# A quarter of the first sequence's probabilities split before it is turned, and turned by DMA transposes

## The reference

```
x = x + layernorm(attn(layernorm(x)))         # attn: q, k with rotary positions,
                                              #   w = softmax(q k^T / sqrt(128)), out = (w v) wo^T
x = x + layernorm(ffn(layernorm(x)))          # ffn, twice: z = z + mixed(rmsnorm(z))
# mixed: router softmax over 8 experts, best 2 of 8, each silu(z w1) * (z w3) @ w2, weighted
```

## Time and profile before

| | |
|---|---|
| median of 3 runs (lowest, highest) | 1055.57 us (1053.36, 1055.62) |
| the profiled execution's own time; its span | 1055.24 us; 1053.5 us |
| mean granted TensorE clock | 0.987 of full |
| PE busy | 994.1 us, 94% |
| DVE, ACT, POOL busy | 692.6, 563.5, 564.4 us |
| chain that ended last | PE 79%, DVE 12% |
| one step of the first sequence | 7.63 us |

### The profile page before, as it was taken

The page is one execution under the profiler, slowest core; times in us unless marked ns, Lnnn a source line. Parts: engine busy times, 40 slices in busy tenths (PEclk is TensorE's granted clock), DMA queues, the critical chain, the costliest instruction groups (busy, mean ns, idle before and its releaser), DMA issues.

```text
span 1053.5 us, 22892 instructions
## 1 busy us (share of the span) xinstructions
PE 994.1 (94%) x7304; PEld 687.3 (65%) x7304; DVE 692.6 (66%) x1511; ACT 563.5 (53%) x1107; POOL 564.4 (54%) x742
## 2 busy tenths in 40 slices
PE   7999998989999899999999999999998999999991
PEld 5678786767788567666666755666755666666661
DVE  7889998989998555684434546635469433575557
ACT  4567676668888645433334566335575333333333
POOL 3335566875788764434444366444376444455435
PEclk9999999999999999999999999999999999999996
DMA  9910000000000245324337534437434433764563
GB/s 310 370 41 0 0 0 1 1 16 21 15 16 16 48 106 119 96 71 106 90 91 178 134 96 132 95 107 178 119 105 119 98 90 92 171 173 118 146 183 133
DMA packets 137498, 105.32 MB, mean 100 GB/s; under 512 B 84673, under 2 KB 124225, under 8 KB 137409
## 3 DMA queue, kind: packets, MB, share of 16 engines
q1 hardware_dynamic: 123776, 66.88, 24.4%
q0 software_dynamic: 13632, 37.24, 12.0%
HBM read 54.27 MB, written 31.20 MB: 81 GB/s over the span
## 4 chain that ended last, share of the span: by engine, by line
PE 79%; DVE 12%; issue 3%; POOL 2%; ACT 2%; DMA 1%; SPq 0%; another core or an unknown queue 0%; ACTq 0%; DVEq 0%; POOLq 0%
PE psum_s L915 32%; PE psum_o L2242 16%; PE psum_s L1679 6%; PE psum_s L2231 6%; PE psum_t L1674 4%; PE psum_o L1719 3%; PE psum_o L1714 3%; PE psum_t L749 2%; DVE arena L1442 2%; PE psum_s L1656 1%; DMA arena<-in_rope 1%; DVE arena L1422 1%; PE psum_t L2206 1%; PE psum_o L1726 1%; PE psum_y L1706 1%
## 5 line engine op out<-in xcount | busy, mean ns | idle before, releaser
L915 PE MATMUL psum_s<-w_all,arena 128*128 x1704 | 391.9, 380 | 3.2 <-issue 2.5
L1886 POOL DMA_INDIRECT token_rows<-arena,result_row_of_row x142 | 147.9, 1041 | 297.5 <-ACT arena L1995 294.4
L915 PEld LDWEIGHTS psum_s<-w_all,arena 128*128 128x128 f16 x1704 | 157.9, 98 | 183.2 <-issue 8.6
L2242 PE MATMUL psum_o<-w_all,arena 128*128 x1704 | 209.4, 273 | 9.3 <-DVE arena L2170 8.7
L900 DVE SCALAR_TENSOR_TENSOR arena<-psum_s,gate_scale,arena 128x512 f32<-128x512 f32 x142 | 106.5, 750 | 162.8 <-ACT arena L894 78.6
L2242 PEld LDWEIGHTS psum_o<-w_all,arena 128*128 128x128 f16 x1704 | 165.1, 98 | 53.4 <-issue 14.4
L2170 DVE TENSOR_TENSOR arena<-psum_s,arena 128x512 f16<-128x512 f32 x142 | 97.9, 689 | 128.7 <-ACT arena L1988 105.9
L1995 ACT ACTIVATE arena<-psum_o 128x256 f32<-128x256 f32 x142 | 54.4, 383 | 217.4 <-PE psum_o L2242 214.5
L876 POOL DMA_INDIRECT arena<-sorted_rows,token_of_row x142 | 139.7, 984 | 46.5 <-issue 40.4
L894 ACT ACTIVATE arena<-psum_s,silu_scale 128x512 f32<-128x512 f32 x142 | 97.6, 687 | 108.7 <-PE psum_s L915 55.2
L1988 ACT ACTIVATE arena<-psum_s 128x512 f16<-128x512 f32 x142 | 84.7, 597 | 29.6 <-PE psum_s L2231 21.7
(11 more groups left out here) (320 smaller groups left out, 1362.8 us busy)
## 6 DMA issues: line engine op xcount, KB each, us to landing
arena<-token_rows SPq DMA_DIRECT2D x64, 256.0 KB, 3.9
w_all<-in_L_ffn_w SPq DMA_DIRECT2D x24, 512.0 KB, 10.0
sorted_rows<-w_all SPq DMA_DIRECT2D x24, 256.0 KB
out<-x_sb SPq DMA_DIRECT2D x7, 512.0 KB, 3.1
arena<-sorted_rows,token_of_row POOLq DMA_INDIRECT x142
arena<-arena SPq DMA_TRANSPOSE x142
token_rows<-arena,result_row_of_row POOLq DMA_INDIRECT x142
x_sb<-in_L_attn_x SPq DMA_DIRECT2D x1, 2048.0 KB, 15.5
```

The costliest lines, as they stand in the source:

```text
L915: last = nc.tensor.matmul(bank, e_xT[:, u, lx * DC + c, :], w_split[:, bass.ds(e * EW + at, FF)], start=(q == 0), stop=(q == 3 * DC - 1))
L1886: nc.gpsimd.indirect_dma_start(rows, bass.IndirectOffsetOnAxis(ap=targets[:, at : at + 1], axis=0), y_row[:, u, :], None).then_inc(s_sent[ ...
L2242: last = nc.tensor.matmul(psum_e, hT[:, lh, c, :], w_split[:, bass.ds(e * EW + at, D)], start=(q == 0), stop=(q == 3 * FC - 1))
```

## The change

**The quarter.** In the first sequence TensorE no longer turns quarter 0. ACT scales it as it stands, once into f16 (hi) and once in place (`quarter_hi`); POOL subtracts (`quarter_lo`); SP turns hi and lo by two DMA transposes of 128 x 512 f16 each into the place that the split quarter had. PE turns quarter 1 alone at the start of a step and multiplies quarter 0 at the end of the step, behind quarter 2. The buffers are single: hi of tile t-1 is written when the transposes of tile t-2 have landed, SP issues the first one when the PV product of tile t-2 is done, and the exponentials of tile t overwrite the probabilities once `quarter_lo` has read them.

```diff
@@ ACT @@
+            def quarter_hi(t):
+                act.wait_ge(s_exp, 2 * t + 1)
+                    act.wait_ge(s_split_T, 32 * t)
+                nc.scalar.activation(probs_split[:, 0, :], probs[:, 0:512], ACT.Copy, scale=P_SCALE).then_inc(s_p_hi, 1)
+                act.wait_ge(s_p_hi, 4 * t + 2)
+                nc.scalar.activation(probs[:, 0:512], probs[:, 0:512], ACT.Copy, scale=P_SCALE).then_inc(s_quarter, 1)
...
@@ POOL @@
+            def quarter_lo(t):
+                pool.wait_ge(s_quarter, t + 1)
+                nc.gpsimd.tensor_tensor(probs_split[:, 1, :], probs[:, 0:512], probs_split[:, 0, :],
+                                        ALU.subtract).then_inc(s_split_lo, 1)
...
@@ SP @@
+            for t in range(NT):
+                for l in range(2):
+                    if l:
+                        sp.wait_ge(s_split_lo, t + 1)
+                    else:
+                        sp.wait_ge(s_p_hi, 4 * t + 2)
+                        if t:
+                            sp.wait_ge(s_pv, t)
+                    sp.dma_start(pT[:, l, 0:512].rearrange("p (g t) -> p g t", g=4), probs_split[:, l, :],
+                                 transpose=True).then_inc(s_split_T, 16)
...
@@ ACT, step @@
+                if turn and first:
+                    p_copy(t - 1, 1)
+                    quarter_hi(t - 1)
...
+                            if first and h == 0:
+                                act.wait_ge(s_split_lo, t)
...
@@ POOL, normalise @@
+                if t < NT - 2:
+                    quarter_lo(t + 2)
...
@@ PE, step @@
-                    for g in range(2):
+                    for g in range(1 if first else 0, 2):
...
+                        pe.wait_ge(s_split_T, 32 * t)
+                        for kc in range(4):
```

**DVE's step, both sequences.** `p_lo` of quarter 0 is gone in the first sequence, and in both sequences oT's low part now stands ahead of the first maximum:

```diff
                 if turn:
-                    p_lo(t - 1, 0)
-                    p_lo(t - 1, 1)
-                if new:
-                    half_max(t, 0)
+                    p_lo(t - 1, 1, first)
                 if fin:
                     dve.wait_ge(s_o_hi, t - 1)
...
                 if new:
+                    half_max(t, 0)
                     half_max(t, 1)
```

```diff
-            for i in range(3):
-                split(FIRST_SPLITS + 2 * i)
+            for i in range(1, 3):
+                split(FIRST_SPLITS + 2 * (i - 1))
...
-                normalise(NT + i, FIRST_SPLITS + 2 * (i + 3) if i < NT - 2 else None)
+                normalise(NT + i, FIRST_SPLITS + 2 * (i + 2) if i < NT - 2 else None)
+                if i == NT - 3:
+                    split(FIRST_SPLITS + 2 * NT)
...
-                if i == NT - 4:
-                    for n in range(UNROLL):
-                        fetch(pool, n)
+                if NT - 4 <= i < NT - 4 + UNROLL:
+                    fetch(pool, i - NT + 4)
```

More of the change, by code:

```diff
@@ L353, in sandwich_kernel @@
         FIRST_SPLITS = SPLITS * (PAIRS - 1)
-        FIRST_ROWS = [(0,), (1, 2), (3, 4)] + [(i + 2,) if i < NT - 2 else () for i in range(3, NT + 4)]
+        FIRST_ROWS = [(), (0,), (1, 2), (3, 4)] + [(i + 1,) if i < NT - 1 else () for i in range(4, NT + 4)]
         PARTS = 2 * NT // MARKED
@@ L1155, in first_row_of, with step @@
                                      scale=factor[:, 0, bass.ds(j, 1)]).then_inc(s_first_row, 1)
-            def step(t, i, new, turn, fin, norm, split, rows=(), routed=False):
-                if turn:
+            def step(t, i, new, turn, fin, norm, split, rows=(), routed=False, first=False):
+                if turn and first:
+                    p_copy(t - 1, 1)
+                    quarter_hi(t - 1)
+                if turn and not first:
                     p_copy(t - 1, 0)
@@ L1443, in half_max, with step @@
                                         ALU.max).then_inc(s_max, 1)
-            def step(t, new, turn, fin, norm, amax, ready=None, inside=None):
+            def step(t, new, turn, fin, norm, amax, ready=None, inside=None, first=False):
+                if turn and not first:
+                    p_lo(t - 1, 0)
                 if turn:
-                    p_lo(t - 1, 0)
-                    p_lo(t - 1, 1)
-                if new:
-                    half_max(t, 0)
+                    p_lo(t - 1, 1, first)
                 if fin:
@@ L1517, in _ @@
             with dve.Fori(3, 11) as i:
-                step(i, True, True, True, True, True)
+                step(i, True, True, True, True, True, first=True)
                 for g in range(2):
@@ L1522, in _ @@
                 first_stats(dve, 0, i - 3)
-            step(11, True, True, True, True, True)
+            step(11, True, True, True, True, True, first=True)
             first_stats(dve, 0, 8)
@@ L1559, in _ @@
             split_lo(7)
-            for i in range(5, PAIRS):
-                split_hi(2 * i - 1)
-                pair(n0 + i, i)
-                split_lo(2 * i - 1)
-            qk_lo(n0 + PAIRS - 1, PAIRS - 1)
+            split_hi(9)
+            pair(n0 + 5, 5)
+            split_lo(9)
+            split_hi(11)
+            pair(n0 + 6, 6)
+            for u in range(2):
+                v_and_rotation(n0 + 7, 7, u)
+            split_lo(11)
+            qk_lo(n0 + 6, 6)
+            split_hi(13)
+            split_lo(13)
+            qk_lo(n0 + 7, 7)
             first_row_variance(dve, link, NT, slice(12, NT))
-            first_factors(dve, link)
             def odd(s):
@@ L1696, in step @@
                     for g in range(2, 4):
-                        pe.wait_ge(s_p_lo, 2 * (t - 1) + g - 1)
+                        if first:
+                            if g == 3:
+                                pe.wait_ge(s_p_lo, 2 * t)
+                        else:
+                            pe.wait_ge(s_p_lo, 2 * (t - 1) + g - 1)
                         turn_p(t - 1, g)
@@ L1708, in step @@
                 if turn:
-                    for kc in range(HALVED):
+                    begin = 4 if first else 0
+                    for kc in range(begin, HALVED):
                         if kc % 4 == 0:
```

123 lines of the change are left out of this document (72 added, 51 removed).

## The result

The changed kernel takes 1070.32 us (median of 4 runs, 1069.64 to 1071.3) against 1054.46 us for the kernel before in the same sitting: ratio 1.015, 95% interval 1.0136 to 1.0164, so 15.9 us slower. I had forecast slower, by 7.1 us. Its profiled execution took 1071.3 us, with a span of 1069.5 us against 1053.5 before: 16.0 us to explain.

The account below looks back on a forecast made before the run. PE looked like the bound, but POOL's chain within each first-sequence step was taken to bind after the change. 15.5 - 1.2 - 2.5 - 6.0 + 1.3 = +7.1 on 1055.24 gave 1062.3 us; 80% range 1047.5 to 1070.

Parts of the forecast that it names:

- POOL's ring: First sequence: POOL's chain through ACT's copies and PE sets the step, 8.4 us instead of 7.63; whole sequence +15.5 us.
- Steps 3 to 11: First sequence: nine steps, each 0.78 us longer, +7.0 us together.
- Step 1: First sequence: ends 0.2 us late, from one more POOL operation and the product one block further behind.
- Steps 12 to 15: First sequence: POOL's root of 1.03 us joins the chain that sets the step; 37.8 us instead of 31.2, +6.6.
- The second ring: First sequence: ACT's copies, DVE's maxima and the exponentials alone need 7.7 us a step, against 7.63 before.
- the other edits: Outside the first sequence: -1.2, -2.5 and -6.0 us of gains and +1.3 us of loss; remaining edits costed at nothing.
- Eight kept-clock matmuls: Before the second sequence's first pair: a half-clock block of 3.50 us would take 2.25; gain 1.2 us (0 to 1.3).
- Router weights: Scaled earlier: PE's 1.30 us wait and part of a half-clock stretch behind it go; gain 2.5 us (1.3 to 3.5).
- Second sequence's start: Maxima 2.2 us earlier, next scores at full clock 1.5, plus earlier rotation and oT's low part; gain 6.0 us (3 to 7).
- Tail: POOL's second weight split, 2.3 us, about half left, delays the last projection and expert tiles; loss 1.3 us (-1 to +4).
- The third: Rival: POOL's chain sets the first sequence's step and the edits elsewhere bring little; 1068 us, chance 0.14.
- The fourth: Rival: PE's 1.2 us wait in each step drops TensorE's clock; one step in four gives +25, 1087 us; chance 0.04.

Follow-up runs that it names:

- Experiment 4: Changed kernel with POOL's cast and low part of quarter 2 moved ahead of the residual addition in the first sequence: 1058.68 us, ratio 1.0038 to the kernel before.
- experiment 6: Kernel of experiment 5 (one ACT copy left out), with PE taking quarter 0's block ahead of quarter 2's: 1048.17 us, ratio 0.997 to the kernel before.
- experiment 11: Changed kernel with the row-variance root of steps 12 to 15 moved ahead of POOL's low part of quarter 0: 1064.19 us, ratio 1.0113 to the kernel before.
- experiment 5: Kernel of Experiment 4 without ACT's second copy of quarter 0, the scaling in place (inexact): 1057.29 us, ratio 1.0013 to the kernel before.
- experiment 1: Changed kernel without the first sequence's part: quarter 0 goes through TensorE again, all other edits stay: 1055.03 us, ratio 1.000 to the kernel before.
- experiment 9: Kernel of experiment 7 with POOL's row-variance root ahead of its last two weight splits: 1052.66 us, ratio 0.9972 to the kernel before.
- Experiments 3: Kernel of experiment 1 with the second sequence's weight splits and gathers back where they stood before: 1053.79 us, ratio 0.9994 to the kernel before.
- 7: Kernel of experiment 1 with the last even weight group's low part made by DVE instead of POOL: 1053.56 us, ratio 0.9987 to the kernel before.
- 8: Kernel of experiment 7 with the three row gathers behind each tile's row shift, not its residual addition: 1050.42 us, ratio 0.9951 to the kernel before.
- experiment 2: Kernel before with only the first sequence's part added (quarter 0 turned by DMA transposes): 1070.56 us, ratio 1.0153 to the kernel before.

## Why the prediction was right in direction and wrong in size

- **First sequence, POOL's ring: right.** 8.27 us a step for a forecast of 8.41, POOL's gapless row, PE's wait of 0.90 ahead of quarter 2's block, and no wait for the transposes but one. Experiment 4 takes the ring away, by order alone, and most of the time with it; experiment 6 takes the rest, with a copy left out. By the starts of the steps the whole sequence cost 17.5 us for a forecast of 15.5. Steps 3 to 11 cost 6.2 (forecast 7.0), step 16 cost 1.6 (1.7). Step 1 cost 0.9 (0.2): its transpose met full DMA engines, which the one transpose of the earlier trace rows did not. The others landed 2.4 us after their issue, in the median, where my estimate of 2.3 came from the figure of the Trainium skill ("DMA: Bandwidth & Descriptors", section "Anatomy of one DMA — SWDGE (gpsimd) path"); that figure is one for DMAs issued from GpSimd, while these are issued by SP. Steps 12 to 15 cost 8.9 (6.6): the root's 1.04 plus a clock that fell behind two of the waits of 1.9 us; experiment 11, which has the root elsewhere, has neither.
- **The second ring: half right.** 7.7 us was forecast for ACT and DVE, and 7.73 is where the step stays without POOL's ring. That the two agree so well is luck in part: from the negated maximum to the exponential it is 0.79 us there, DVE being held beside POOL's subtraction, for 0.51 in the sum, and smaller pieces elsewhere make up for it. And experiment 5 shows that without the scaling copy a third ring holds 7.59, through PE's turning of quarter 2, ACT, POOL and both blocks. Quarter 0's block stands last in the change, and I had not asked what that does to the step's end.
- **The step that failed: the other edits, forecast -8.4, measured 0.0** (experiment 1, within 1.5 us). Two of its four terms were mis-sized, the start of the second sequence and the tail; together with 2 us more in the first sequence they are the difference between 7.1 and 15.9. The terms:
  - Eight kept-clock matmuls: forecast -1.2; from the first turning to the second pair's block 6.59 us for 8.12, -1.5. Right.
  - Router weights: forecast -2.5; the rest of the pairs gave -1.4 (2.9 less 1.5), a part of which belongs to the earlier rotation. The wait of 1.30 went, but DVE held PE 1.45 us later on, at 211.23.
  - **Second sequence's start: forecast -6.0, measured -1.6** (in scores 0 to 15). The clock's 1.5 came (step 1: 7.82 us for 9.26). The 2.2 for the earlier maxima came as 0.7 (and so the exponential 0.7 us sooner behind its scores, not 3 to 4): I let DVE's small instructions keep the lengths of before, where POOL was idle beside them, while the change put POOL's splits there; experiment 9 gives back 1.1 of that in step 0. Steps 2 and 3, for which I had no cost, take 0.9 more; ACT waits 2.46 us for POOL there, with two routed rows in one step, so I put it down to the routed rows, but no run has them apart.
  - **Tail: forecast +1.3, measured +5.1.** I halved the second split's 2.3 us. It took 3.0 (1.36 + 1.64) and a gather of 1.24 (with its 0.17 of issue) stood behind it, all on the way to the row factors, and the two waits brought the half clock. Experiments 3, 7 and 8 take 4.8, 4.2 and 5.5 us of it back. My own bound, "the upper end if the clock falls in the wait", was the case.
- **The rivals.** The third, the ring and little gain elsewhere, at 1068, came nearest: the gains stayed small, and the tail cost 5.1 where it had 4. It had a chance of 0.14. The fourth (the clock swings in every step) did not come: beside waits of 0.9 us it is 1.00 in the rows from 60 to 135 us. The Trainium skill's rule that I weighed there ("TensorE: Matmul & The Clock Gate", section "A second HAM failure mode") is borne out only behind longer waits: of those of 1.9 us, two of three here and one of three in experiment 2, and the two of about 2 us in the tail.

## What to carry to other kernels

Work taken from the busiest engine gains only if the rings around it have slack: write down each ring of one step, with every instruction in its issue order, and ask of each new piece whether it could stand behind the one that others wait for (here that order was worth 11.6 us). An edit that moves work from one place to another has two prices; cost both by the waits of the receiving place, or the gain at one end is counted and the loss at the other halved. Small DVE instructions on SBUF operands can be held until the POOL instruction beside them ends, so their lengths must be read where POOL is as busy as it will be.

## What the runs showed that I had not expected

- A DVE instruction of 4 elements per partition takes 0.15 to 0.16 us beside an idle POOL and up to 1.00 beside POOL's two-operand instructions, and it ends with them; the negated maximum, one element, took 0.22 to 1.10. POOL's own pieces are longer too where DVE's two-operand instructions of 512 columns (L1444) run beside them: 1.36 and 1.64 us in the tail for 1.04 and 1.16.
- A DMA transpose of 128 KB landed 2.4 us after its issue in the median, and 5.0 and 3.5 us after it where the DMA engines were full.
- Waits of 0.9 us in each step of 8.3 left PE's clock at 1.00 for 75 us; waits of 1.9 were followed by a half clock in two steps of three, and in one of three in experiment 2.
